# The last group's closing sum in PSUM: two products per block instead of a transposition and a vector sum

## The reference, cut to what matters

```python
x = _layernorm(x + _L0_gnn_ref(x, adj, ...))
x = _layernorm(x + _L1_gnn_ref(x, adj, ...))
x = _layernorm(x + _L2_gnn_ref(x, adj, ...))
x = _layernorm(x + _L3_gnn_ref(x, adj, ...))      # 32 batches x 256 nodes x 128 features

def _L3_gnn_ref(...):
    h = relu(adj @ (x @ Wg0 + bg0)); h = relu(adj @ (h @ Wg1 + bg1))
    for p in range(1, 5):          # an LSTM over windows of p nodes; the window's last node
        ...                        # takes the last hidden state
    return h
def _layernorm(x, eps=1e-05):
    m = mean(x); v = var(x)        # over the 128 features
    return (x - m) / sqrt(v + eps)
```

## Time and profile before

| what | us |
| --- | --- |
| median of 3 runs (lowest, highest) | 624.95 (624.62, 625.41) |
| the profiled execution's own time | 624.48 |
| its span, first to last instruction or transfer | 622.7 |
| TensorE busy | 605.8 (97%) |
| DVE busy | 473.1 (76%) |
| ACT busy | 434.3 (70%) |
| POOL busy | 207.9 (33%) |

### The profile page before, as it was taken

How to read it: one execution, slowest core, us unless ns; L and a number is a source line. 1 busy time by engine, 2 the same in 40 slices (tenths; PEclk the granted TensorE clock), 3 DMA queues, 4 the chain that set the end, 5 groups by cost and what they waited for, 6 DMA issues and landing times.

```text
span 622.7 us, 9523 instructions
## 1 busy us (share of the span) xinstructions
PE 605.8 (97%) x2614; PEld 419.7 (67%) x2614; DVE 473.1 (76%) x1623; ACT 434.3 (70%) x1000; POOL 207.9 (33%) x324
## 2 busy tenths in 40 slices
PE   9999999999999999999999999999999999999994
PEld 5646556447875687578668757865885686576794
DVE  4999999876947767876878788778868876465666
ACT  3668776956947775795777668567947775556774
POOL 1365551005332043227404540740373064003301
PEclk9999999999999999999999999999999999999998
DMA  8334000000000010001001100100010010000000
GB/s 337 145 126 170 1 2 0 0 1 2 1 2 1 0 35 1 2 11 58 1 2 30 39 1 2 35 35 1 20 49 2 0 35 35 0 2 34 2 35 34
DMA packets 8981, 20.00 MB, mean 32 GB/s; under 512 B 2016, under 2 KB 5088, under 8 KB 8800
## 3 DMA queue, kind: packets, MB, share of 16 engines
q1 hardware_dynamic: 8928, 19.40, 8.7%
HBM read 12.05 MB, written 4.19 MB: 26 GB/s over the span
## 4 chain that ended last, share of the span: by engine, by line
PE 76%; ACT 4%; DVE 3%; issue 2%; POOL 1%; POOLq 0%; ACTq 0%; DVEq 0%
PE QQ L898 27%; PE QQ L910 15%; PE PA L881 4%; PE PA L853 4%; PE PB L872 2%; PE PB L863 2%; PE PB L731 2%; PE PA L731 2%; PE PA L833 2%; PE PB L833 2%; PE QQ L932 1%; PE PA L684 1%; PE PA L844 1%; PE PB L951 1%; PE QQ L942 1%
## 5 line engine op out<-in xcount | busy, mean ns | idle before, releaser
L1273 ACT ACTIVATE raw<-QQ,BL 128x256 f32<-128x256 f32 (+2 forms) x279 | 150.1, 558 | 69.6 <-PE QQ L898 36.9
L898 PE MATMUL QQ<-HT,WT 128*128 128x256 f32 (+2 forms) x558 | 183.5, 473 | 0.8 <-DVE HT L1792 0.4
L898 PEld LDWEIGHTS QQ<-HT,WT 128*128 128x128 f32 x558 | 103.9, 190 | 58.2 <-issue 29.7
L475 POOL TENSOR_TENSOR RSD<-VAR,pw 128x4 f32<-128x4 f32 (+1 forms) x43 | 61.8, 1437 | 175.9 <-DVE VAR L1498 175.5
L910 PE MATMUL QQ<-HB,WT 128*128 128x256 f32 (+2 forms) x336 | 100.8, 443 | 0.4 <-DVE HB L1792 0.2
L554 POOL COPY HB<-HB 32x256 f32<-32x256 f32 x96 | 42.9, 447 | 150.0 <-DVE HB L1685 144.8
L910 PEld LDWEIGHTS QQ<-HB,WT 128*128 128x128 f32 x336 | 61.1, 190 | 30.9 <-issue 13.4
L1309 ACT ACTIVATE raw<-raw 128x256 f32<-128x256 f32 (+4 forms) x79 | 37.1, 470 | 30.2 <-DVE raw L1774 25.8
L1764 DVE SCALAR_TENSOR_TENSOR raw<-raw 128x256 f32<-128x256 f32 (+2 forms) x60 | 31.6, 527 | 15.7 <-ACT raw L1273 15.1
L1792 DVE SCALAR_TENSOR_TENSOR HB<-raw 128x256 f32<-128x256 f32 (+4 forms) x42 | 20.3, 483 | 23.6 <-ACT raw L1309 23.6
L1108 ACT ACTIVATE X<-Z,OFF,RSD 128x128 f32<-128x128 f32 x80 | 31.8, 482 | 2.5 <-POOL OFF L481 2.5
(11 more groups left out here) (254 smaller groups left out, 1157.6 us busy)
## 6 DMA issues: line engine op xcount, KB each, us to landing
four<-in_x SPq DMA_DIRECT2D x8, 512.0 KB, 3.8
raw<-in_xt SPq DMA_DIRECT2D x8, 512.0 KB, 6.4
out<-four SPq DMA_DIRECT2D x7, 512.0 KB, 2.6
HB<-HB SPq DMA_DIRECT2D x96, 32.0 KB, 1.8
WT<-in_lstm SPq DMA_DIRECT2D x1, 2048.0 KB, 8.0
later<-in_later SPq DMA_DIRECT2D x1, 725.5 KB, 10.2
AD<-in_adj SPq DMA_DIRECT2D x2, 256.0 KB, 4.5
out<-four SPq DMA_DIRECT2D x2, 256.0 KB, 2.0
```

The source lines that it names most:

```text
L475: pool.tensor_tensor(RSD[kk][:, ts], VAR[kk][:, ts], pw[:, ts], ALU.pow).then_inc(ln[k]["rstd"], some)
L898: mm = pe.matmul(steps_view(Q[q], k), WT[:, 0, (p - 1) * 4 + q, :], ht_view(par, k), start=True, stop=(s == 0))
L1273: act.activation(TG[q][:, at:n], Q[q][:, at:n], ACT.Tanh, scale=0.5 if q == G else 0.25, bias=BL[:, p - 1, q:q + 1]).then_inc(g_ok, 1)
```

## The change

It concerns the last group alone, after its last LSTM step.

- TensorE: in place of four transpositions per half, `t_residual_half` puts the residual `X1` into two of the lane's banks by two products with the identity (128 columns into bank G, 384 columns into bank I, `start=True`), and `t_added_half` adds `HT^T` x `HALF` by four products onto it, where `HALF` is the identity times 0.5. The result in PSUM is the residual sum itself. The eight constant products between the halves are gone.
- DVE: `t_sum_half` is gone, both times. The statistics read the banks, and so do the three scalings of the second half.
- ACT: its five scalings read the banks.
- POOL: one instruction more, which makes `HALF` (in `late`, part of the tensor HB) after the last but one group's scaling and ahead of the last group's RSD; it signals `half_ident`, for which TensorE waits.
- Of each half, tile b = 0 lies in bank G and tiles 1 to 3 in bank I, so ACT (tile 4) and DVE (tiles 5 to 7) read different banks of the second half.

The diff, with what only names things left out:

```diff
+        HALF = late[:, 1, 0:P]
...
+        def last_tile(t):
+
+            b = t % GB
+            return lanes[t // GB].banks[I if b else G][:, b * P:(b + 1) * P]
...
                 if g == GROUPS - 1:
+                    pool.wait_ge(px_ps, GB * (GROUPS - 2))
+                    pool.tensor_scalar(HALF, ident[:], 0.5, 0.0, ALU.mult, ALU.add).then_inc(half_ident, 1)
                     rstd(3, 2, g, 0)
...
-            def t_turn_half(par, c):
+            def t_residual_half(c):
                 v = lanes[c]
+                pe.wait_ge(v.ok, lane_gate(c, NSTEP - 1, G))
+                for q, a, b in ((G, 0, 1), (I, 1, GB)):
+                    pe.matmul(v.banks[q][:, a * P:b * P], ident[:], X1[:, LAST, c * BANK + a * P:c * BANK + b * P], start=True, stop=False)
+
+            def t_added_half(par, c):
+                v = lanes[c]
+                pe.wait_ge(half_ident, 1)
                 pe.wait_ge(v.h, v.step0 + NSTEP - LANED)
                 for b in range(GB):
-                    mm = pe.transpose(v.banks[I][:, b * P:(b + 1) * P], by_batch(HT[:, par])[:, b, c * P:(c + 1) * P], ident[:])
+                    mm = pe.matmul(last_tile(c * GB + b), by_batch(HT[:, par])[:, b, c * P:(c + 1) * P], HALF,
+                                   start=False, stop=(b in (0, GB - 1)))
                 mm.then_inc(half_ps, 1)
...
-                    t_turn_half(par, 0)
-                    spin(Q[F][:, 0:P], 8)
-                    t_turn_half(par, 1)
+                    t_residual_half(0)
+                    t_added_half(par, 0)
+                    t_residual_half(1)
+                    t_added_half(par, 1)
...
-                act.activation(OUT[:, 1, t * P:(t + 1) * P], ZF[:, t * P:(t + 1) * P], ACT.Identity, bias=OFF[2][:, t:t + 1],
+                act.activation(OUT[:, 1, t * P:(t + 1) * P], last_tile(t), ACT.Identity, bias=OFF[2][:, t:t + 1],
...
-            def t_sum_half(c):
-                cols = slice(c * BANK, (c + 1) * BANK)
+            def t_norm_half(c):
                 dve.wait_ge(half_ps, c + 1)
-                reach(dve, ln[3]["out"], TILES * LAST)
-                dve.scalar_tensor_tensor(out=ZF[:, cols], in0=lanes[c].banks[I], scalar=0.5, in1=X1[:, LAST, cols],
-                                         op0=ALU.mult, op1=ALU.add).then_inc(zf_ok, 1)
-
-            def t_norm_half(c):
-                dve.wait_ge(zf_ok, LAST + 1 + c)
-                norm_stats(3, 2, ZF, LAST, c)
+                for t in range(c * GB, (c + 1) * GB):
+                    dve.bn_stats(STL[2][:, t, :], last_tile(t)).then_inc(ln[3]["stats"], 1)
+                norm_small(3, 2, LAST, c)
...
-                            t_sum_half(0) if (k, l) == (NSTEP - 1, 1) else None
...
-                    t_sum_half(1)
...
-                dve.tensor_scalar(OUT[:, 1, t * P:(t + 1) * P], ZF[:, t * P:(t + 1) * P], MEAN[2][:, t:t + 1],
+                dve.tensor_scalar(OUT[:, 1, t * P:(t + 1) * P], last_tile(t), MEAN[2][:, t:t + 1],
```

More of the change, by code:

```diff
@@ L388, in build @@
                   + [(i, h) for i in range(AHEAD, NCHUNK) for h in range(HC)])
-        half_ps = sem("half_ps")
+        half_ps, half_ident = sem("half_ps"), sem("half_ident")
         gate_x, gate_c = sem("gate_x"), sem("gate_c")
```

## The result

| | us, median (lowest, highest) | runs |
| --- | --- | --- |
| before | 624.81 (624.46, 625.46) | 22 |
| after | 625.89 (625.16, 626.27) | 22 |

The ratio is 1.0014, 95% interval 1.0008 to 1.0020. The change costs about 0.9 us by this ratio (1.08 between the two medians), where 0.67 us had been forecast as a gain, and 625.89 lies above the range, which ended at 625.1.

What follows compares the result with a forecast made beforehand. DVE's queue, not TensorE, was taken to bound the tail. Second statistics earlier by 0.79 us and transfers costing 0.12 summed to -0.67 us, giving 624.3 from a median of 624.95; range 623.6 to 625.1.

Steps and rivals of the forecast that it cites:

- Is TensorE in time for that?: TensorE's residuals and added products in the tail: 0.87 and 0.90 us each, ending at 615.18 as now, before DVE wants them.
- the slack of 0.35: Second half: TensorE's last result at 615.18, DVE ready for the second statistics at 615.53, so 0.35 us to spare.
- the slack of 0.5 us: First half: TensorE's last result at 613.35, first statistics beginning at 613.86, so 0.5 us to spare.
- Rival C: Second half's added products: TensorE becomes the bound, every pace doubling if the clock fell to its lower level; 627.4 us, 3%.
- weaker form: Milder case of Rival C: one more wait of some 0.5 us on TensorE's path, giving 624.5, inside the range.
- The two sums: DVE's vector sums removed: gains of 0.08 us for the first and 0.73 us for the second.
- The residual: TensorE's products putting X1 into the banks: 0.87 us per half, a row of 384 columns taking 486 ns.
- rival A: DVE's PSUM reads cost 59 ns more in eight statistics, 0.15 us more in three scalings: 624.9 us, 10%.
- ACT's scaling: ACT's last scaling in the second half: 458 ns from PSUM against 490 from SBUF, a gain of 0.03 us.
- DVE's scalings: DVE's three scalings of the second half: 351 ns each from PSUM against 341 from SBUF, +0.01 to +0.03 us.
- The transfers: The last two output transfers, issued closer together, share the DMA engines: +0.12 us, bounds 0 and 0.2.
- rival B: Last transfers: the second's data wait until the first has landed, nearly all of the 0.79 us lost; 624.9 us, 8%.

Runs made afterwards that it cites:

- e1: Changed kernel with the added products' weights loaded from 128 neighbouring columns of HT instead of every fourth: 624.05 us against 624.85 for the kernel before, ratio 0.9988.
- e6: Kernel before without the eight constant products between the two halves' transpositions: 624.84 us against 625.06, ratio 0.9997.
- e4: Changed kernel with each tile made by transposing HT, then adding twice the residual by a product, epsilon times four: 624.45 us against 624.85 for the kernel before, ratio 0.9993.
- e5: As e4, but TensorE signals after tile 0 and again after tile 3 of each half: 624.23 us against 625.06 for the kernel before, ratio 0.9987.
- e7: Changed kernel with the added products' weights taken from every second column of HT (8 bytes apart) instead of every fourth: 624.38 us, one run.
- e9: Changed kernel with the added products' weights taken from every third column of HT (12 bytes apart) instead of every fourth: 624.89 us, one run.
- e8: Changed kernel with the added products' weights taken from every eighth column of X1 (32 bytes apart), finished long before, instead of HT's every fourth: 626.16 us, one run.
- e2: Changed kernel with operands exchanged in the added products: identity as weights, strided HT streamed, no transposition or factor 0.5: 625.17 us, one run.

## Why the prediction was wrong, step by step

**The step that failed is "Is TensorE in time for that?"**, its term for the added products: 0.90 us for eight rows, at a pace of 0.112 us. That pace was read from L942 and L872, whose weights lie together, and carried over to products whose weights are every fourth column of `HT`. Measured were 0.243 us. It hit twice. Lane 0's products ended their stream 1.05 us late, and since the list of TensorE has no gap left, the second residual and lane 1's products began 615.59 - 611.66 = 3.93 us after the reference point instead of 2.97. Then these took 617.48 - 615.59 = 1.89 us instead of 1.06. Together TensorE's last result came 0.96 + 0.83 = 1.79 us late; the slack of 0.35 took its part, and 1.44 us reached the statistics. They were in fact 5.87 - 4.38 = 1.49 us late.

The same term also used up the slack of 0.5 us that the prediction gives the first half. The first statistics begin at 614.92, after 0.45 us of idle time that TensorE ended, 614.92 - 611.66 = 3.26 us after the reference point instead of 613.86 - 611.15 = 2.71. By this alone DVE would have come to the second statistics 0.55 us late, at 4.93 instead of 4.38. TensorE's second lateness was the larger and hid it.

**The evidence at hand.** The strided load was in the trace of before, and it was not free. The prediction used, 0.56 us for four loads of L959, only as a time at which loading may begin. The same load stands 56 times in L951, and beside it stand transpositions whose weights lie together (L744):

```profile
L744 PEld LDWEIGHTS PA<-ident,HB x48: 140/141/143, 185.2 to 466.4; 128*128 128x128 f32 x48
L951 PEld LDWEIGHTS PB<-ident,HT x56: 196/211/212, 244.5 to 573.8; 128*128 128x128 f32 x56
```

A load with columns 16 bytes apart took 211 ns instead of 141, 70 more. Carried over to the added products as an estimate, 70 ns on each of eight rows are 0.56 us, more than the slack of 0.35 and of 0.5. That would have been a warning, not the size: in a product the load took 137 ns more (329 against 192), and the pace of the rows doubled, while a transposition's rows follow each other by 0.119 us instead of 0.110 (L951, L744). No row of before shows this operand in a product. The term had no bound of its own, and the range had no room for it.

**Rival C** had the place right (the second half's added products, TensorE as the bound) and the point of decision: it gave 28% more than the predicted stretch of 3.81 us, and the stretch became 617.48 - 611.89 = 5.59 us, 47% more. Its mechanism was wrong: the granted clock stayed at 1.00. Its "weaker form" of half a microsecond was priced at 624.5 and so dismissed; the true excess was three times that. 3% was too little for a stretch whose pace came from other instructions.

**Terms that held.**
- The two sums: with TensorE out of the way (e1) the statistics begin at 4.40 us against 4.38 forecast.
- The residual: 0.87 us, and 487 ns for the row of 384 columns against 486 worked out between the earlier trace rows.
- Statistics from PSUM: 281 ns (L1891) as in the earlier trace rows; of rival A this part falls.
- ACT's scaling: 456 ns from PSUM, 458 forecast (479 from SBUF, L1411).
- The constant products: nothing (e6). POOL's `HALF`: nothing seen; e1 makes it too and has the forecast start of the statistics.

**Terms that were off, without deciding anything.**
- DVE's scalings were forecast at 341 to 351 ns and take 404:

```profile
L2003 DVE TENSOR_SCALAR four<-PA,MEAN,RSD x3: 402/404/411, 620.4 to 621.1; 128x128 f32<-128x128 f32 x3
```

  The row L1604 was "of the same kind" only by name: it reads one scalar from memory, L2003 reads two; whether that is the reason, no run shows. Against the same instruction from SBUF (341) it is 63 ns more. The three end 0.19 us later than they would have, and they are now the last ahead of the second transfer, where before ACT's was. The rule of the Trainium skill that the prediction weighed (page VectorE: DVE Perf Modes, section "The TRN2 errata") would make it 65 ns, an estimate from its cycles: the scalings, 63 ns, agree with it, the statistics, 5 ns, do not. So rival A was right for three instructions of eleven.
- The transfers were to lose 0.12 us to each other. They lose nothing. From the second issue to the end of the span it is 2.49 us before, where the issues lie 1.33 apart, and 2.47 in e1, where they lie 0.80 apart. The stretches of e1 in which the one and then the other moves (same columns as above):

```profile
619.42:620.14 0.72, 0.00 (x0) 0.00 (x0) 0.00 (x0) 0.00 (x0) 0.00 (x0) 0.50 0.92 347
620.23:620.90 0.67, 0.00 (x0) 0.00 (x0) 0.00 (x0) 0.00 (x0) 0.00 (x0) 0.50 0.94 358
```

  The first has moved its data within some 0.75 us, just before the second starts, so rival B falls. The issues lie 0.80 apart instead of the 0.6 forecast, for two reasons: the first comes at 618.63 - 611.08 = 7.55 us, 0.12 earlier than forecast, since ACT's first four scalings take 1.51 us instead of 1.65, and the second at 8.35, 0.08 later than forecast. (Of the 0.18 us by which DVE's scalings end late, 0.10 do not arrive, because the issue follows them after 0.03 us and not after 0.1.) What happens below 0.75 was not seen. Against the forecast the second issue is 0.08 us late and the way from there to the end 2.47 instead of 2.61, 0.14 short; so the end of e1, 0.06 from the forecast, owes something to luck.

**What stays open.** That the distance is the cause is shown; why it costs is not. The model with pieces of 16 bytes fits the five distances and is no more than argued. Why a transposition pays 70 ns a load and hardly any pace, where a product pays 137 ns and twice the pace, no run shows. The streaming side of a transposition was not tried with a stride.

## What to carry to other kernels

A pace belongs to an instruction together with its operands' layout, not to the instruction alone: before a TensorE product is put in the place of a transposition, ask how far apart the columns of its operands lie, and take the price from a row with that stride in that kind of instruction, or give it a bound of its own. If the stride occurs in another kind of instruction, compare it there with the same instruction without the stride: a difference is a warning. When a layout can't be changed, let a transposition carry the strided operand and a product the contiguous one; both can accumulate in the same tile (e4, e5). And when work is taken off the engine that bounds a tail, work out the other engine's stretch with its own worst row: its slack here was 0.35 us of 3.81, less than what the doubling of one term (0.90 us) costs.

## What the runs showed of the hardware

- A float32 load of 128x128 weights for a product took 192 ns with columns 4 bytes apart, 196 at 8, 261 at 12, 329 at 16, 335 at 32 (e1, e7, e9, after, e8). The products' rows took 275, 281, 338, 397, 402 ns, and followed each other by 0.111, 0.118, 0.176, 0.233, 0.238 us.
- A streamed float32 operand with columns 16 bytes apart took 406 ns a row (e2), against 275.
- A transposition's load took 141 ns with columns 4 bytes apart (L744, before) and 211 with columns 16 bytes apart (L951, before); 198 in e4.
- DVE read PSUM instead of SBUF at 5 ns more in the statistics (276 to 281) and 63 ns more in a scaling with two scalars from memory (341 to 404). ACT's scaling took 23 ns less from PSUM than from SBUF (479 to 456).
- Two transfers of 256 KB issued 0.80 us apart took no longer than two issued 1.33 apart: 2.47 us from the second issue to the end, against 2.49 (e1, before).
